# Expert weights split block by block, TensorE working on blocks i, i-2 and i-4, and a residual that stays resident

## What is computed

```python
x = x + time_and_channel_mix(layernorm(x), ...)       # layernorms, scan over 1024 steps, FFN 256-1024-256
# x is the residual from here
xt = layernorm(x).reshape(-1, 256)                    # N = 8192
gates = sigmoid(einsum('nd,ed->ne', xt, expert_sel))  # 32 experts
sel_val, sel_idx = top_k(gates, 4)
scores = relu(einsum('nd,edf->nef', xt, keys))        # 256 -> 128 per expert
scores = scores * gate_full[:, :, None]               # zero but for the 4 chosen
out = x + einsum('nef,efv->nv', scores, values)       # 128 -> 256 per expert
```

## Time and profile before

| | us |
|---|---|
| median of 3 runs | 1602.18 (1601.1 to 1603.06) |
| profiled execution | 1615.93, its span 1614.1 |
| mix phase, from 0 | to about 900 |
| expert phase | about 900 to 1482 |
| combine phase | about 1482 to the end |
| busy shares of the span | PE 72%, DVE 65%, ACT 46%, POOL 54% |

### The profile page before, as it was taken

The page is one execution under the profiler, slowest core; times in us unless marked ns, Lnnn a source line. Parts: engine busy times, 40 slices in busy tenths (PEclk is TensorE's granted clock), DMA queues, the critical chain, the costliest instruction groups (busy, mean ns, idle before and its releaser), DMA issues. The chain is left out here.

```text
span 1614.1 us, 28314 instructions
## 1 busy us (share of the span) xinstructions
PE 1161.0 (72%) x7399; PEld 1046.6 (65%) x7400; DVE 1042.1 (65%) x2424; ACT 737.4 (46%) x1393; POOL 864.9 (54%) x935
## 2 busy tenths in 40 slices
PE   6799999999999999999751476766776677673000
PEld 5688888888887888888651466666666666663000
DVE  4878888787887787887547344444444444443877
ACT  3655667555676556676342244333434343432000
POOL 0524676766676766675636355555555555553000
PEclk9899999999999999999875688888888878887555
DMA  5000221221221121221535644444444444435999
GB/s 184 14 27 10 71 77 63 73 70 42 72 75 62 69 69 46 72 73 54 198 128 217 191 141 139 140 138 140 134 144 140 136 139 143 136 105 177 381 365 333
DMA packets 101917, 201.25 MB, mean 125 GB/s; under 512 B 16983, under 2 KB 49901, under 8 KB 100464
## 3 DMA queue, kind: packets, MB, share of 16 engines
q1 hardware_dynamic: 63216, 120.34, 23.9%
q0 software_dynamic: 27648, 67.70, 11.5%
q10 hardware_dynamic: 11008, 12.65, 2.2%
HBM read 105.28 MB, written 103.71 MB: 129 GB/s over the span
## 5 line engine op out<-in xcount | busy, mean ns | idle before, releaser
L1359 POOL DMA_INDIRECT expert_rows<-y,dest x320 | 318.1, 994 | 267.5 <-issue 238.0
L1127 POOL DMA_INDIRECT lists<-rows,slot x256 | 301.1, 1176 | 74.5 <-issue 70.8
L1269 PE MATMUL ps<-xt_hi,keys 128*128 128x256 f32 x640 | 184.2, 347 | 138.1 <-issue 120.9
L1336 DVE TENSOR_TENSOR xt_lo<-ps,xt_hi 128x512 fp32r<-128x512 f32 x160 | 110.3, 690 | 210.8 <-ACT xt_hi L1296 126.8
L1269 PEld LDWEIGHTS ps<-xt_hi,keys 128*128 128x128 f32 x640 | 134.6, 231 | 153.6 <-issue 152.8
L1296 ACT ACTIVATE xt_hi<-ps 128x512 fp32r<-128x512 f32 x160 | 96.7, 604 | 140.5 <-PE ps L1256 95.6
L859 DVE TENSOR_TENSOR k_lo<-ksq,k_hi 128x512 fp32r<-128x512 f32 x128 | 100.6, 813 | 85.9 <-ACT k_hi L652 65.4
L1308 ACT ACTIVATE y<-ps 128x512 f32<-128x512 f32 x160 | 96.0, 600 | 131.0 <-PE ps L1284 84.6
L535 PE MATMUL ps<-wv_hi,k_hi 128*128 128x256 f32 x512 | 146.0, 285 | 0.0
L537 PE MATMUL ps<-wv_lo,k_hi 128*128 128x256 f32 x512 | 144.8, 283 | 0.0
L539 PE MATMUL ps<-wv_hi,k_lo 128*128 128x256 f32 x512 | 144.8, 283 | 0.0
(11 more groups left out here) (201 smaller groups left out, 3461.2 us busy)
## 6 DMA issues: line engine op xcount, KB each, us to landing
xr<-lists SPq DMA_DIRECT2D x160, 260.0 KB
ye<-expert_rows SPq DMA_DIRECT2D x32, 1024.0 KB, 8.1
x_sb<-in_x SPq DMA_DIRECT2D x16, 512.0 KB
residual<-xp SPq DMA_DIRECT2D x16, 512.0 KB, 4.6
experts_raw<-in_expert_in SPq DMA_DIRECT2D x8, 1024.0 KB, 22.5
lists<-zeros SPq DMA_DIRECT2D x25, 260.0 KB, 10.9
expert_rows<-y,dest POOLq DMA_INDIRECT x320
resid<-residual SPq DMA_DIRECT2D x20, 256.0 KB, 5.6
```

Source lines behind the costliest of these rows:

```text
L1127: pool.indirect_dma_start(lists, bass.IndirectOffsetOnAxis(ap=slot[:, q, n:n + 1], axis=0), rows[:, q, n // TOPK, :], None).then_inc(scatt ...
L1269: mm = pe.matmul(ps[:, H + q, 0:BLOCK], keys[:, (r - 1) % SLOTS, half, k * DE:(k + 1) * DE], m[:, q, k, :], start=n == 0, stop=n == 3 * KD ...
L1336: dve.tensor_tensor(xt_lo[:, q].rearrange("p k b -> p (k b)"), ps[:, XT + q, :], xt_hi[:, q].rearrange("p k b -> p (k b)").bitcast(F32), A ...
L1359: pool.indirect_dma_start(expert_rows, bass.IndirectOffsetOnAxis(ap=dest[:, r, s:s + 1], axis=0), y[:, r, s, :], None, bounds_check=OUT_RO ...
```

## The change

- The weights are no longer split in mix. At the end of step i of the expert loop ACT copies the 512 columns of block i's expert, rounded, from `experts_raw` into `w` (new L1307), and DVE subtracts to get the lo half (new L1345). `w` has 4 slots. The key copy of DVE is gone; H and Y read `w`. `experts_w` is gone; SP waits at the end of mix that the raw weights have landed.
- PE works on T(i), H(i-2) and Y(i-4). XT has 4 banks; H and Y keep 2. T(i) waits `x_ready` for block i-4. xt and h have 4 slots.
- SP, ACT and DVE read eight plan entries at once at the head of a ring; the reads per block and PE's read are gone.
- `resid` (8.4 MB, all 8192 rows) takes the place of `experts_w` in SBUF; ACT loads it with 4 DMAs behind the first ring. `resid_head` is gone. Combine has `ye` 8 deep, no loads of the residual, and no wait for `stored` in its loop.

```diff
-        experts_w = nc.alloc_sbuf_tensor_at("experts_w", [P, 2, E, W], F32R, offset=arena_at)
         experts_raw = nc.alloc_sbuf_tensor_at("experts_raw", [P, E, W], F32, offset=arena_at + HALF)
+        resid = nc.alloc_sbuf_tensor_at("resid", [P, N // P, D], F32, offset=arena_at)
...
                 square(0)
-                if last:
-                    round_experts(0, 5)
...
-                if last:
-                    round_experts(5, LOADS)
-
-            def round_experts(first, end):
-                act.wait_ge(val_ready, NT)
-                for n in range(first, end):
-                    act.wait_ge(experts_loaded[n], 16)
-                    act.activation(experts_w[:, 0, part(n), :], experts_raw[:, part(n), :],
-                                   ACT.Copy).then_inc(experts_rounded, 1)
...
-            def split_experts(first, end):
-                for n in range(first, end):
-                    dve.wait_ge(experts_rounded, n + 1)
-                    dve.tensor_tensor(experts_w[:, 1, part(n), :], experts_raw[:, part(n), :],
-                                      experts_w[:, 0, part(n), :].bitcast(F32),
-                                      ALU.subtract).then_inc(experts_split, 1)
...
-                if isinstance(t, int) and V == NT - 1:
-                    split_experts(0, 4)
...
-    w = g["experts_w"]
     SLOTS = RING // 2
-    keys = sb("keys", [P, SLOTS, 2, KD * DE], F32R)
+    H_LAG, Y_LAG = 2, 4
+    HBANKS, YBANKS = 2, 2
+    KEYS = KD * DE
+    w = sb("w", [P, SLOTS, 2, W], F32R)
...
-    xt_hi, xt_lo = (sb(f"xt_{h}", [P, 2, KD, BLOCK], F32R) for h in ("hi", "lo"))
-    h_hi, h_lo = (sb(f"h_{h}", [P, 2, BLOCK], F32R) for h in ("hi", "lo"))
+    xt_hi, xt_lo = (sb(f"xt_{h}", [P, SLOTS, KD, BLOCK], F32R) for h in ("hi", "lo"))
+    h_hi, h_lo = (sb(f"h_{h}", [P, SLOTS, BLOCK], F32R) for h in ("hi", "lo"))
...
-    XT, H, Y = 0, 2, 4
+    XT, H, Y = 0, SLOTS, SLOTS + HBANKS
...
+    def loop(eng, step, drain=0, plan=None, behind_first=None):
+
+        def one(ring):
+            values = None
+            if plan is not None:
+                table, top = plan
+                _, values = nc.values_load_multi_w_load_instructions(
+                    table[0:1, bass.ds(ring * RING, RING)], engines=(eng.engine,), min_val=0, max_val=top)
+            for r in range(RING):
...
+
+        one(0)
+        if behind_first:
+            behind_first()
...
+            one(ring)
         for i in range(NBLOCKS, NBLOCKS + drain):
-            step(i, i % RING, i // RING)
+            step(i, i % RING, i // RING, None)
...
                 after(sp, mark_ready, i - SLOTS + 1)
-                row = sp.value_load(plan_row[0:1, bass.ds(i, 1)], min_val=0, max_val=LIST_ROWS - BLOCK)
-                sp.dma_start(xr[:, r % SLOTS], lists[bass.ds(row, BLOCK), :].rearrange("(p s) c -> p s c", p=P)
...
                              ).then_inc(rows_loaded[r % SLOTS], 16)
 
-            loop(sp, step)
-            sp.dma_start(g["resid_head"][:], g["residual"][0:HEAD * P, :].rearrange("(g p) d -> p g d", p=P)
...
+            loop(sp, step, plan=(plan_row, LIST_ROWS - BLOCK))
...
-                if not isinstance(i, int) or i < NBLOCKS:
+            def step(i, r, ring, _):
+                if enters(i):
                     pe.wait_ge(rows_loaded[r % SLOTS], 16 * (2 * ring + r // SLOTS + 1))
-                    after(pe, x_ready, i - 1)
+                    after(pe, x_ready, i - SLOTS + 1)
                     for k in range(KD):
                         for s in range(SUB):
-                            mm = pe.transpose(ps[:, XT + r % 2, k * BLOCK + s * P:k * BLOCK + (s + 1) * P],
+                            mm = pe.transpose(ps[:, XT + r % SLOTS, k * BLOCK + s * P:k * BLOCK + (s + 1) * P],
...
-                if not isinstance(i, int) or i >= 2:
-                    e = pe.value_load(plan_expert[0:1, bass.ds(i - 2, 1)], min_val=0, max_val=E - 1)
-                q = (r - 1) % 2
-                if not isinstance(i, int) or 1 <= i <= NBLOCKS:
-                    pe.wait_ge(keys_ready, i)
-                    pe.wait_ge(x_ready, i)
-                    after(pe, h_ready, i - 2)
+                if lagging(i, H_LAG):
...
+                    pe.wait_ge(w_ready, b + 1)
+                    pe.wait_ge(x_ready, b + 1)
+                    after(pe, h_ready, b - HBANKS + 1)
...
-                                           keys[:, (r - 1) % SLOTS, half, k * DE:(k + 1) * DE],
+                            mm = pe.matmul(ps[:, H + q % HBANKS, 0:BLOCK],
+                                           w[:, q, half, k * DE:(k + 1) * DE],
...
-                q = (r - 2) % 2
-                if not isinstance(i, int) or i >= 2:
-                    pe.wait_ge(h_ready, i - 1)
-                    after(pe, ycopy_ready, i - 3)
...
+                if lagging(i, Y_LAG):
+                    b, q = i - Y_LAG, (r - Y_LAG) % SLOTS
+                    pe.wait_ge(h_ready, b + 1)
+                    after(pe, ycopy_ready, b - YBANKS + 1)
+                    v_hi, v_lo = (w[:, q, half, KEYS:] for half in (0, 1))
...
                     mm.then_inc(y_done, 1)
 
-            loop(pe, step, drain=2)
+            loop(pe, step, drain=Y_LAG)
...
-            def step(i, r, ring):
-                q = r % 2
-                if not isinstance(i, int) or i < NBLOCKS:
+            def step(i, r, ring, expert):
+                if enters(i):
+                    q = r % SLOTS
                     act.wait_ge(xt_done, i + 1)
-                    after(act, h_done, i - 1)
+                    after(act, h_done, i - SLOTS + 1)
...
-                if not isinstance(i, int) or 1 <= i <= NBLOCKS:
-                    act.wait_ge(h_done, i)
-                    after(act, y_done, i - 2)
-                    act.activation(h_hi[:, q, :], ps[:, H + q, 0:BLOCK], ACT.Relu).then_inc(hhi_ready, 1)
-                q = (r - 2) % 2
...
-                    after(act, sent[b], 16 * SUB * (ring - 1 if r >= 2 else ring - 2) + 16 * SUB)
-                    act.activation(y[:, b].rearrange("p s d -> p (s d)"), ps[:, Y + q, :],
+                if lagging(i, H_LAG):
+                    b, q = i - H_LAG, (r - H_LAG) % SLOTS
+                    act.wait_ge(h_done, b + 1)
+                    after(act, y_done, b - SLOTS + 1)
...
+                if lagging(i, Y_LAG):
+                    b, q = i - Y_LAG, (r - Y_LAG) % RING
+                    act.wait_ge(y_done, b + 1)
+                    after(act, sent[q], 16 * SUB * (ring if r >= Y_LAG else ring - 1))
+                    act.activation(y[:, q].rearrange("p s d -> p (s d)"), ps[:, Y + q % YBANKS, :],
...
+                if enters(i):
+                    q = r % SLOTS
+                    after(act, y_done, i - SLOTS + 1)
+                    act.activation(w[:, q, 0, :], raw[:, bass.ds(expert[r], 1), :].rearrange("p a w -> p (a w)"),
+                                   ACT.Copy).then_inc(whi_ready, 1)
+
+            def load_residual():
+                for n in range(PIECES):
+                    act.dma_start(resid[:, n * PIECE:(n + 1) * PIECE, :],
+                                  residual[n * PIECE * P:(n + 1) * PIECE * P, :]
+                                  .rearrange("(g p) d -> p g d", p=P)).then_inc(resid_loaded, 16)
+
+            loop(act, step, drain=Y_LAG, plan=(plan_expert, E - 1), behind_first=load_residual)
+            act.wait_ge(resid_loaded, 16 * PIECES)
...
-                    after(dve, h_done, i - SLOTS + 1)
-                    dve.tensor_copy(keys[:, r % SLOTS], w[:, :, bass.ds(expert[r], 1), 0:KD * DE].rearrange(
-                        "p h a w -> p (h a) w").bitcast(F32)).then_inc(keys_ready, 1)
-
-
...
-                    if r < RING - 1:
-                        load_expert(i + 1, r + 1)
...
-            loop(dve, step, drain=1)
+                    q = r % SLOTS
+                    dve.wait_ge(whi_ready, i + 1)
+                    dve.tensor_tensor(w[:, q, 1, :], raw[:, bass.ds(expert[r], 1), :].rearrange("p a w -> p (a w)"),
+                                      w[:, q, 0, :].bitcast(F32), ALU.subtract).then_inc(w_ready, 1)
+
+            loop(dve, step, drain=H_LAG, plan=(plan_expert, E - 1))
...
-    DEPTH = 4
+    DEPTH = 8
     ye = scope.enter_context(nc.sbuf_tensor("ye", [P, DEPTH, GROUPS, TOPK, D], F32))
-    resid = scope.enter_context(nc.sbuf_tensor("resid", [P, DEPTH, GROUPS, D], F32))
     ye_loaded = [sem(f"ye_loaded_{r}") for r in range(DEPTH)]
-    stored = [sem(f"stored_{r}") for r in range(DEPTH)]
-    resid_loaded = [sem(f"resid_loaded_{r}") for r in range(DEPTH)]
+    stored = sem("stored")
...
+            def step(i, r, ring):
                 tokens = GROUPS * P
                 after(sp, sum_step, ADDS * (i - DEPTH + 1))
...
-                if not head:
-                    after(sp, stored[r], 16 * ring)
-                    sp.dma_start(resid[:, r], residual[bass.ds(i * tokens, tokens), :]
```

(13 more changed lines are left out.)

94 lines of the change are left out of this document (37 added, 57 removed).

## The result

Medians of five and five runs: before 1602.18 us, changed 1586.26 us; ratio 0.9902, 95% interval 0.9881 to 0.9923. The changed kernel is 1% faster, and it took 15.9 us off, where 48.8 were forecast. So the two profiles differ by 38.6 us and the medians by 15.9: 22.7 us of the miss are in the choice of the two executions, which I had carried over as if it were a constant.

A forecast was written before the change was run, and what follows sets the result against it. The expert phase was taken as a loop of waits, with PE's signals held during POOL's scatters. Seven terms summed to -48.8 us: 1615.9 to 1567.1 profiled, 1602.2 to 1553.4 median; 8-in-10 range 1440 to 1604.

The forecast's parts named there:

- Mix tail: End of mix: without weight rounding ACT's last x3t copies start at about 843.8, saving 6.8 us; bounds 0 and -9.1.
- Combine: Combine phase: 32 steps at 3.25 us, 111.9 us against 131.7, saving 20 us; bounds 0 and -22.
- fourth rival: Combine: DMA engines, not DVE, hold it near 4.2 us a step, so no saving there, 1573 us; chance 0.10.
- Pauses: Expert phase: longer POOL bursts leave 46 pauses, 18 fewer, at 2.7 us each, saving 49 us; bounds 0 and -173.
- step 3: Expert phase: deeper PE pipeline adds one block per POOL burst, 3.5 in place of 2.5, saving 49 us.
- Filling: Expert phase, filling and draining: two more steps before the first y cost 6 us; bounds +3 and +8.
- Plan reads: Expert phase: eight plan entries read ahead of every ring, 2.6 us each time, cost 8 us; bounds 0 and +50.
- Holds: Expert phase: DVE's new subtraction with two SBUF inputs holds POOL's scatters, costing 10 us; upper end 69 or 109.
- third rival: Expert phase: each subtraction holds a scatter its whole 0.69 us, 109 us and not 10, 1652 us; chance 0.08.
- Residual: Expert phase: loading 8.4 MB in place of 3.1 costs 3 us; bounds 0 and 21.
- term 2: Combine phase: steps of 3.25 us paced by DVE's additions, saving 20 us; bounds 0 and -22.
- first rival: Expert phase: scatters hold no signals; four banks remove the pauses and POOL bounds, -173 not -49, 1429 us; chance 0.15.

## Why the forecast was wrong

1. *Mix tail, -6.8.* Measured -0.6 on record, -7.9 on chip 7. The chain was right (x3t directly behind the transposes). The lower bound of 0 had named the reason: the zero fill ends the phase, and on record its issues stretched over 38.2 us in place of 30.9 when they started earlier.
2. *Combine, -20.* Measured -22.0 and -19.2. Right, with its reason; the fourth rival fell.
3. *Pauses, -49.* Measured -73. The count came out as forecast, 3.5 blocks a burst and 45 pauses (the residual's among them) for 46, but for another reason than the one given: with the holds gone a burst has 2.7 blocks, so the depth had at most 0.3 of the block that step 3 credited to it. The two traces compared may be of different chips. The match is luck. The 24 us beyond the term are mostly in shorter pauses: 2.1 us on the mean without the residual's, before 2.6, where I had kept 2.7. On a short chip there is nothing to save.
4. *Filling, +6.* Measured +1.5 and +1.7.
5. *Plan reads, +8.* No gap shows on POOL every 8 blocks; on chip 7 its scatters run without one. On POOL they are hidden. DVE waits at a ring's head for 2.8 us (56.8 us over 20 times), near my 2.6.
6. *Holds, +10.* Measured +38 in the scatters on record, inside the bound of 69, but nearly four times the term. (The third rival's 0.69 x 160 is 110 and not 109, which changes nothing.) On a long chip they are given back by the pauses; on chip 7 14.8 are paid.
7. *Residual, +3.* Measured +17.0 and +17.3. This is the term that failed on every chip. I had bounded the data by 21 us and charged 3 since they lie beside other work; I had not seen that the issues of the second to fourth DMA of 2 MB hold the engine that issues them, here ACT, for whose copy POOL waits. That they wait for the DMAs ahead of them in the queue is my reading; what is shown is that 16 issues of 512 KB, a ring apart, do not.

By the record's own profiles the sum was 48.8 against 38.6, of which 7 stands for 14 of error and 1 for 6; 3 to 6 hide each other (-24, -4.5, -8 and +28 against the forecast), so that the sum of the profiles came out this near is luck as well. The rest of the miss, 22.7 of 32.9 us, is the step before the sum: "I carry the difference over". One profiled execution 13.75 us above its median is not a base to which a constant applies; the executions of the changed kernel alone span 14 us (1577.4 to 1591.2). It also lies 12 us above the longest of the five timed executions of its kernel on record, and 3.4 above the longest of seven on chip 0, so it may well come from another chip or hour than they. By the medians the terms of mix and the expert phase, -28.8 in the forecast, came to about nothing (the estimate in the first section), and term 2 is the whole saving. In which phase the record's profile of before was longer than its other executions stays open, since no second profile of it on a long chip was taken.

The largest thing was not in the forecast as a mechanism of the chip at all. The first rival had the short chips' world, POOL as the bound and no pauses, but as something that the change would bring. It is there before the change, where the rule of the Trainium skill ("TensorE: Matmul & The Clock Gate", section "The cost: per-tile semaphore tail") and the trace agree: 0.04 us from PE to ACT. On long chips the trace disagrees, with 2.8 us. The third rival's rule, of the Trainium skill ("SBUF — State Buffer", section "Who interferes with whom"), is borne out in kind on both: scatters of 1.37 to 1.46 us beside the subtraction with two SBUF inputs, means of 1.004 and 0.990 us without it. It does not give the size: beside the subtractions of 256 columns, which also have two SBUF inputs, the mean is 1.010. The price is due only on short chips.

Open: what holds PE's signals on a long chip, indirect DMAs or any traffic; what sets 3.5 to 3.6 us a block there, which holds, keys and burst length hardly move; and whether depth alone helps there. The runs for the first and the last met short chips only, and a kernel without any store of the expert rows was never timed. The record's trace of before speaks against a scatter alone being enough: in its mix phase only 9 of 140 of PE's signals given inside a burst of POOL's scatters came over 0.3 us late, against 218 of 319 in the expert phase.

## What to carry to other kernels

Before you cost a stall that one trace shows, see whether it is there in a second execution on another chip; a change that pays only by removing it can turn its sign. Look at what the issue of a large DMA does to the engine that issues it: here pieces of 512 KB a ring apart cost 0.43 us each, three of 2 MB in a row 15 to 19 us. An engine on which nothing waits would be the other way, untried here. Count bursts and pauses over the whole phase before you explain them from one stretch. A time lost on the engine that seems the bound is a cost only while nothing else sets the pace: take it away alone and look.

## What was not expected of the hardware

- One program takes 1450 us on four chips and 1610 us on another; in the profiled executions 152 of 163 us are in the expert phase, where PE's completion signals come 0.014 us after the matmul at the median, or in 268 of 439 cases over 0.3 and up to 5.5 us.
- Issuing three DMAs of 2 MB held ACT 15.4 us (18.5 on chip 7), one of 512 KB 0.43.
- On a long chip, scatters made 38.5 us shorter left the loop 10 us longer.
- A two-input subtraction of 512 columns beside the scatters makes their mean 1.110 us; cut into two of 256 columns, 1.010.
